# Attention scores of a 16-head layer as one matmul per head on 32-row tiles

## The reference, cut to what matters

```
mod = silu(c) @ ada_w.T + ada_b          # shifts, scales, gates
h = layernorm(x) * (1 + scale_msa) + shift_msa
q, k, v = (h @ qkv_w.T + qkv_b)          # 16 heads of 8 each
attn = einsum('bhnd,bhmd->bhnm', q, k) * 8 ** -0.5
attn = where(mask, attn, -1e9);  attn = softmax(attn)
x = x + gate_msa * (einsum('bhnm,bhmd->bhnd', attn, v) @ proj_w.T + proj_b)
x = x + gate_mlp * (gelu(modulate(layernorm(x)) @ fc1_w.T + fc1_b) @ fc2_w.T + fc2_b)
```

## Time and profile before

| | |
|---|---|
| three runs | 249.68, 250.20, 250.73 us |
| span of the profiled execution | 249.0 us |
| TensorE matmul busy | 206.9 us (83%) |
| VectorE busy | 186.8 us (75%) |
| ScalarE busy | 180.2 us (72%) |
| GpSimd busy | 163.5 us (66%) |
| granted TensorE clock | 0.998 of full speed |
| attention steps | about 72 to 213 us |

### The profile page before, as it was taken

The page is one execution under the profiler, slowest core; times in us unless marked ns, Lnnn a source line. Parts: engine busy times, 40 slices in busy tenths (PEclk is TensorE's granted clock), DMA queues, the critical chain, the costliest instruction groups (busy, mean ns, idle before and its releaser), DMA issues.

```text
span 249.0 us, 5248 instructions
## 1 busy us (share of the span) xinstructions
PE 206.9 (83%) x1596; PEld 154.1 (62%) x1596; DVE 186.8 (75%) x530; ACT 180.2 (72%) x381; POOL 163.5 (66%) x287
## 2 busy tenths in 40 slices
PE   0689998999998687977978787897888778998894
PEld 0548875678876466755746655665666556564784
DVE  0673895647199998989989989989998999058514
ACT  2147769545758788997998988989899877984330
POOL 2499589998676586875876776677689723338500
PEclk9999999999999999999999999999999999999999
DMA  6950000071000000000000000000000000000112
GB/s 159 413 219 0 4 1 0 5 295 42 0 4 0 0 3 1 4 1 0 0 0 0 0 0 0 0 0 0 0 0 3 0 0 3 0 3 0 42 42 86
DMA packets 2768, 8.28 MB, mean 33 GB/s; under 512 B 496, under 2 KB 832, under 8 KB 2496
## 3 DMA queue, kind: packets, MB, share of 16 engines
q1 hardware_dynamic: 2176, 6.22, 6.7%
q10 hardware_dynamic: 576, 1.86, 2.0%
HBM read 7.01 MB, written 1.06 MB: 32 GB/s over the span
## 4 chain that ended last, share of the span: by engine, by line
DVE 34%; PE 31%; issue 19%; ACT 6%; POOL 5%; DMA 2%; DVEq 1%; POOLq 0%; ACTq 0%
PE ps L305 8%; DVE nmax L938 7%; PE ps L295 7%; DVE kdiag L933 7%; DVE nmdiag L956 5%; PE ps L253 3%; DVE xn L781 3%; PE ps L353 2%; PE ps L241 2%; DMA xs<-x 2%; DVE nm L946 2%; PE ps L364 2%; DVE bn_c L979 2%; POOL rstd L1080 2%; DVE qk L923 2%
## 5 line engine op out<-in xcount | busy, mean ns | idle before, releaser
L665 ACT ACTIVATE qdiag<-qxT 32x512 fp32r<-32x512 f32 x64 | 40.2, 628 | 1.4
L938 DVE TENSOR_REDUCE nmax<-ps 128x8 f32<-128x1024 f32 x32 | 37.7, 1217 | 2.2 <-PE ps L353 1.6
L670 ACT ACTIVATE shared<-ps 128x1024 f32<-128x1024 f32 x32 | 31.0, 1021 | 6.6 <-PE ps L377 6.6
L353 PE MATMUL ps<-kdiag,qxT 128*128 128x512 f32 x64 | 20.5, 436 | 16.2 <-DVE kdiag L933 16.2
L1209 POOL TENSOR_TENSOR qkx<-qk,qkx 128x256 fp32r<-128x256 f32 x32 | 22.8, 734 | 16.3 <-ACT qkx L650 16.2
L1214 POOL TENSOR_TENSOR kdiag<-kxT,quarter 128x512 fp32r<-128x512 f32 x16 | 19.9, 1244 | 19.4 <-ACT kxT L659 19.4
L621 ACT ACTIVATE hid<-ps,W 128x512 f32<-128x512 f32 x32 | 21.6, 691 | 14.7 <-PE ps L295 14.6
L933 DVE CAST kdiag<-kxT 32x512 fp32r<-32x512 f32 x48 | 31.2, 651 | 1.0 <-ACT kxT L659 0.6
L305 PE MATMUL ps<-W,hid 128*128 128x128 f32 x256 | 29.9, 275 | 0.0
L305 PEld LDWEIGHTS ps<-W,hid 128*128 128x128 f32 x256 | 29.4, 192 | 0.6 <-issue 0.5
L295 PE MATMUL ps<-hT,W 128*128 128x512 f32 x64 | 29.4, 598 | 0.0
(11 more groups left out here) (148 smaller groups left out, 477.8 us busy)
## 6 DMA issues: line engine op xcount, KB each, us to landing
gate<-gates SPq DMA_DIRECT2D x1, 2048.0 KB, 6.9
xs<-x SPq DMA_DIRECT2D x4, 256.0 KB, 9.4
mask_i<-mask ACTq DMA_DIRECT2D x1, 1024.0 KB, 9.5
W<-weights SPq DMA_DIRECT2D x1, 768.0 KB, 12.0
out<-xs SPq DMA_DIRECT2D x3, 256.0 KB, 2.3
R<-rows ACTq DMA_DIRECT2D x1, 512.0 KB, 7.0
W<-weights SPq DMA_DIRECT2D x1, 512.0 KB, 10.8
W<-weights SPq DMA_DIRECT2D x1, 392.0 KB, 10.1
```

Source lines behind the costliest of these rows:

```text
L353: ins = mm(ps[:, t, :], qxT[u][:, t], kdiag[u][:, t], start=True, stop=True)
L665: ins = a(qdiag[u][rows, :, r], qxT[u][rows], ACT.Copy)
L670: a(pT[u][:, 2 * e:2 * e + 2], ps[:, 2 * e:2 * e + 2, :].rearrange("n t (r q) -> n t r q", r=4), ACT.Exp, scale=HD ** -0.5).then_inc(s["c_ ...
L938: v.tensor_reduce(nmax[u][:, 8 * e:8 * e + 8], ps[:, 2 * e:2 * e + 2, :].rearrange("n t (r k) -> n (t r) k", r=4), AX.X, ALU.max, negate=T ...
```

## The change

Each head gets a matmul of its own. The operands are the 32 rows of the head in `qxT` and `kxT` themselves, so `kdiag`, `qdiag` and `nmdiag` aren't built, and their copies, memsets and waits go. A matmul with 32 rows uses a tile of 32 rows of the array. Row group r writes to bank r (before, slice t wrote to bank t), and so the maxima, the exponentials, the v slots and the host's packing of the v bias and the projection weights take the heads in another order. All sixteen score matmuls now stand behind one wait for both halves of the exponentials of b-1; before, banks 0 and 1 waited for the first half alone, and `front_a` stood between the two halves. The four `nmdiag` copies become one copy `nmT` of 128 rows, and the subtraction's first half signals ScalarE by itself.

```
-                for t in (t for e in halves for t in (2 * e, 2 * e + 1)):
-                    if back and t % 2 == 0:
-                        pe.wait_ge(s["c_exp"], 2 * b + t // 2 - 1)
-                    ins = mm(ps[:, t, :], qxT[u][:, t], kdiag[u][:, t], start=True, stop=True)
-                    if t % 2:
-                        ins.then_inc(s["c_S"], 1)
+                if back:
+                    pe.wait_ge(s["c_exp"], 2 * b)
+                for t in range(4):
+                    for r in range(4):
+                        rows = slice(32 * r, 32 * r + 32)
+                        ins = mm(bank(r)[:, t], qxT[u][rows, t], kxT[u][rows, t], start=True, stop=True,
+                                 skip_group_check=True)
+                        if t == 3 and r % 2:
+                            ins.then_inc(s["c_S"], 1)
...
-                for t in (2 * e, 2 * e + 1):
-                    mm(ps[:, t, :], kxT[u][:, t], qdiag[u][:, t], start=True, stop=False, skip_group_check=True)
+                for t in range(4):
+                    for r in (2 * e, 2 * e + 1):
+                        rows = slice(32 * r, 32 * r + 32)
+                        mm(bank(r)[:, t], kxT[u][rows, t], qxT[u][rows, t], start=(t == 0), stop=False,
+                           skip_group_check=True)
...
+                pe.wait_ge(s["c_nmT"], b + 1)
                 for e in range(2):
-                    pe.wait_ge(s["c_nmT"], 2 * b + e + 1)
                     for t in range(4):
-                        ins = mm(bank(t)[:, 2 * e:2 * e + 2], sel[:, t], nmdiag[u][:, 2 * e:2 * e + 2], start=False,
-                                 stop=True, skip_group_check=True)
-                        if e and t % 2:
-                            ins.then_inc(s["c_ST"], 1)
+                        for r in (2 * e, 2 * e + 1):
+                            rows = slice(32 * r, 32 * r + 32)
+                            ins = mm(bank(r)[:, t], sel[rows, t], nmT[u][rows], start=False, stop=True,
+                                     skip_group_check=True)
+                    ins.then_inc(s["c_ST"], 1)
...
-                scores(b, u, (0,), back)
                 if ahead:
                     front_a(b + 2, u)
-                scores(b, u, (1,), back)
+                scores(b, u, back)
...
-            def front_qdiag(b, u, rs):
-                act.wait_ge(s["c_qT"], b + 1)
-                for r in rs:
-                    rows = slice(32 * r, 32 * r + 32)
-                    ins = a(qdiag[u][rows, :, r], qxT[u][rows], ACT.Copy)
-                ins.then_inc(s["c_qd"], 1)
...
-            def front_kdiag(b, u):
-                dve.wait_ge(s["c_kT"], b + 1)
-                for r in range(3):
-                    rows = slice(32 * r, 32 * r + 32)
-                    ins = v.tensor_copy(kdiag[u][rows, :, r], kxT[u][rows])
-                ins.then_inc(s["c_kd"], 1)
...
-                for r in range(4):
-                    rows = slice(32 * r, 32 * r + 32)
-                    ins = v.tensor_copy(nmdiag[u][rows, r], ps[rows, 4, 256:256 + N])
-                    if r % 2:
-                        ins.then_inc(s["c_nmT"], 1)
+                v.tensor_copy(nmT[u][:], ps[:, 4, 256:256 + N]).then_inc(s["c_nmT"], 1)
...
-            for m in qdiag:
-                p.memset(m[:].bitcast(F32), 0.0).then_inc(s["diag_ok"], 1)
...
-            def front_kdiag(b, u):
-                pool.wait_ge(s["c_kT"], b + 1)
-                p.tensor_tensor(kdiag[u][:, :, 3], kxT[u][:], quarter[:].unsqueeze(1).broadcast_to((128, 4, N)), ALU.mult)\
-                    .then_inc(s["c_kd3"], 1)
```

More of the change, by code:

```diff
@@ L143, in build @@
         kxT = [sb(f"kxT{u}", [128, 4, N], F32R) for u in range(2)]
-        qdiag = [sb(f"qdiag{u}", [128, 4, 4, N], F32R) for u in range(2)]
-        kdiag = [sb(f"kdiag{u}", [128, 4, 4, N], F32R) for u in range(2)]
         vx = [sb(f"vx{u}", [N, 8 * 64]) for u in range(2)]
@@ L148, in build @@
         nm = [sb(f"nm{u}", [N, 4, 32]) for u in range(2)]
-        nmdiag = [sb(f"nmdiag{u}", [128, 4, N], F32R) for u in range(2)]
+        nmT = [sb(f"nmT{u}", [128, N], F32R) for u in range(2)]
         pT = [shared[:, 4 * u:4 * u + 4] for u in range(2)]
@@ L342, in front_k, with scores @@
                 ins.then_inc(s["c_Tk"], 1)
[L344 to L349, removed]
-                for t in (t for e in halves for t in (2 * e, 2 * e + 1)):
-                    if back and t % 2 == 0:
-                        pe.wait_ge(s["c_exp"], 2 * b + t // 2 - 1)
-                    ins = mm(ps[:, t, :], qxT[u][:, t], kdiag[u][:, t], start=True, stop=True)
-                    if t % 2:
-                        ins.then_inc(s["c_S"], 1)
+            def scores(b, u, back):
+                pe.wait_ge(s["c_qT"], b + 1)
+                pe.wait_ge(s["c_kT"], b + 1)
+                if back:
[7 more added lines that the diff above has]
+                            ins.then_inc(s["c_S"], 1)
             def scores_t(b, u, e):
-                if e == 0:
-                    pe.wait_ge(s["c_kT"], b + 1)
-                    pe.wait_ge(s["c_qd"], 3 * b + 3)
                 pe.wait_ge(s["c_max"], 2 * b + e + 1)
-                for t in (2 * e, 2 * e + 1):
-                    mm(ps[:, t, :], kxT[u][:, t], qdiag[u][:, t], start=True, stop=False, skip_group_check=True)
+                for t in range(4):
[3 more added lines that the diff above has]
+                           skip_group_check=True)
             def turn_maxima(b, u):
@@ L1007, in step @@
                     statistics_1(b - 2)
-                if front:
-                    front_kdiag(b + 1, 1 - u)
                 if ahead:
@@ L1119, in _ @@
                 p.memset(nm[u][:], 0.0).then_inc(s["c_vinit"], 1)
-                p.memset(nmdiag[u][:].bitcast(F32), 0.0).then_inc(s["c_vinit"], 1)
-            pool.wait_ge(s["c_vinit"], 6)
+            pool.wait_ge(s["c_vinit"], 4)
             for u in range(2):
@@ L1166, in _, with prepare @@
                 .then_inc(s["own_ok"], 1)
-            for m in kdiag:
-                p.memset(m[:].bitcast(F32), 0.0).then_inc(s["diag_ok"], 1)
-            def prepare(b, u, end=False, last_kdiag=False):
+            def prepare(b, u, end=False):
                 settled(pool)
@@ L1232, in step @@
                 if ahead:
-                    prepare(b + 2, u, end, True)
+                    prepare(b + 2, u, end)
                 else:
@@ L1302, in columns, with heads @@
         return np.concatenate([cols, np.zeros((128, 16 - cols.shape[1]), np.float32)], axis=1)
+    def heads(rows):
+        return rows.reshape(4, 2, 2 * HD, -1).transpose(1, 0, 2, 3).reshape(rows.shape)
     packed = {
@@ L1310 @@
         "ada": l1["ada_w"].T,
-        "cols1": columns(l1["ada_b"], l1["qkv_b"][2 * C:], l1["fc1_b"]),
+        "cols1": columns(l1["ada_b"], heads(l1["qkv_b"][2 * C:]), l1["fc1_b"]),
         "qkv": l1["qkv_w"].T,
-        "proj1": l1["proj_w"].T, "fc1": l1["fc1_w"].T,
+        "proj1": heads(l1["proj_w"].T), "fc1": l1["fc1_w"].T,
         "fc2": l1["fc2_w"].T.reshape(FC, 128, C).transpose(1, 0, 2).reshape(128, F),
```

36 lines of the change are left out of this document (12 added, 24 removed).

## The result

The changed kernel takes 275.53 us (median of four runs, 270.92 to 277.10), the one before 250.24 beside it. The ratio, 1.0904 of before (95% interval 1.0816 to 1.0992), is taken from the two faster of the four, 270.92 and 274.89; with the median of all four it would be 1.10. Forecast was 243.0 with 234 to 256, so both the sign and the range are wrong. The profiled execution took 274.89 us, with a span of 273.2.

A forecast was written before the change was run, and what follows sets the result against it. VectorE was taken as the bound; relieved, a serial loop of 8.45 us a step against 8.82 remains. Savings 3.7 + 0.8 + 2.0 + 0.8 = 7.3 us give 243 us, range 234 to 256.

The forecast's parts named there:

- The bound: Attention loop before the change: VectorE, busy 16.54 of 17.60 us over two steps, sets the pace.
- Sixteen score matmuls: First scores on TensorE: side-by-side loads on four row tiles, 0.65 to 0.70 us; 1.77 if every load queues.
- Transpose to subtraction: Loop, from the start of the maxima's transpose to the subtraction's start: 1.12 us before plus 0.30 for three shape changes, 1.42.
- The step: One attention step of the loop after the change: 8.45 us against 8.82 before.
- The head: Before the loop: memsets and waits go, first maxima 1.3 us earlier at 71.95, step 1's at 81.2; gain 2.0 us.
- The end: Last step and tail: three `nmdiag` copies less at 0.29, one change of shape more; gain 0.8 us.
- The last paragraph: List of signs to check; a granted clock below full, from TensorE idling longer, would show the forecast wrong.
- the two small operations: Loop, VectorE after the maxima: high and low part of the maxima, 1.02 us.
- Rival A: Weight loads of different row groups queue on TensorE: 10.4 us a step, 272 us; chance 0.15.
- Rival B: Shape changes at 0.27 us each, or TensorE's order, eat the gain: 8.95 a step, 250 us; chance 0.15 with D.
- Rival C: Shape changes free and the two small operations 0.69 us in the loop: 7.8 a step, 235 us; chance 0.20.
- D: No effect, because VectorE wasn't the bound: 250 us; chance 0.15 together with B.

The follow-up runs named there:

- the whole filler: Changed kernel plus eight full-height 128x128 matmuls a step, result unused: four before the scores, four before the transpose of the maxima; 253.77 us, ratio 1.0114.
- half the filler: Changed kernel plus only four unused full-height matmuls a step, those before the scores; 257.44, 260.67, 270.37 and 274.51 us in four runs.
- filling the start alone: Changed kernel plus eight unused full-height matmuls a step in steps 0 and 1 only; 266.25 and 277.26 us beside 250.35.

## Why the prediction was wrong

**The bound, right.** VectorE set the step; without the copies the kernel takes 233 us.

**The loop's terms at full clock, right in the main.** Sixteen score matmuls take 0.67 us in step 0, against 0.65 to 0.70 forecast; queued would be 1.77. Loads for different row groups run side by side. Transpose to subtraction: 1.41 in step 0 (75.89 to 77.30), against 1.42; with the whole filler 1.63. The step: 8.49, 8.65 and 8.58 at full clock with half the filler, against 8.45.

**The head, a mis-sized term.** The first maxima start at 72.89, 0.33 us earlier than before and not 1.3 (71.95 was forecast). The wait for `xn` is gone, as forecast, but the copy of the transposed weights, forecast to end at 41.55, ends at 42.30, and TensorE waits 1.79 us for it. With the memsets gone GpSimd converts the mask earlier (1.90 us from 39.79), and beside it the two small VectorE operations ahead of the copy take 0.81 and 1.83 us where they took 0.16 each; that the one slows the other isn't tested. Step 1's maxima start at 81.76, against 81.2. The end, from the last step's first maxima on, is 44.5 us against 44.05 before, where 0.8 less was forecast; its first 3.3 us run at the low clock. Head and tail together are 1.8 of the 31.5 us that the forecast of the span is short.

**The step that failed** is the sum's silent premise, that every duration read before the change holds after it. The last paragraph named it ("a granted clock below full [...] it stands at 1.00 throughout now") as what would make the forecast wrong, but gave it no price, no chance and no rival. The reason it named, longer idle time, fits the first fall at most; the falls in the loop come without it, and filling the start alone didn't help. Its price can be read from the loop step above, forecast against measured: sixteen scores and their release 0.69 against 1.15, transpose of the maxima after their negation 0.15 against 1.47, transpose to subtraction 1.42 against 1.68, the two small operations 1.02 against 0.81, and 0.02 less in the release of ScalarE; together 1.81 more, 10.26 instead of 8.45. With two steps at 12.4 and twelve near 10.2, the fourteen intervals between the steps' maxima take 146.9 us (81.76 to 228.67), where the forecast had 117.2 (121.73 - 3.7 - 0.8): 29.7 of the 31.5 us between the span forecast (241.7) and the span measured. With the clock restored by filler the kernel takes 253.8, and what then stands above the forecast is in TensorE's order, 8.97 a step.

**Rival A**, 272 us, comes near the time and is refuted as a cause: it needed 1.1 us more for the scores at full clock, and they take 0.67. The forecast gave 0.15 to a case with the right size for a wrong reason. **Rival B**: the transpose starts at 75.89, the tiles behind it at 76.12, so 0.23 from start to start, beside 0.10 within one shape: a change of shape costs 0.13, near the forecast's 0.10 and not B's 0.27. B's 8.95 a step is seen only with the whole filler, which makes the transpose wait. **Rival C**: little came free. The two small operations take 0.81 in the loop and not 1.02, yet the steps at full clock take 8.2 to 8.65 with half the filler, not 7.8. **D** is refuted by the kernel without copies.

**What stays open.** The runs show that tiles of 32 rows hold the clock less well than full-height matmuls, and that it gets worse with their number. By what measure the chip decides isn't shown. Number and kind aren't separated either: 16 are always the first scores, and 32 the transposed scores and the subtraction. Nor was it tried whether the 32-column tiles of the weighted sum, which both kernels have, count in the same way.

## What to carry to other kernels

When full-height matmuls are replaced by small tiles, treat the granted clock as a term of the sum: price the stage at the low level too, as a rival with a chance. Then change the part that relieves the engine that bounds and leave the rest at full height; here a third of the tiles gave 3.3%, 5.8% with one copy moved, and all of them lost 9%. After a surprise look at the clock row of the page before any line of the timeline.

## What was not expected of the hardware

- TensorE can be busy 80 of 80 us by the records and be granted 0.52 of its clock, and the clock can fall with no pause before it (3.00 of 3 us busy from 120 us in the changed kernel); eight matmuls of 128 rows a step in place of eight of 32 rows are worth 87 us.
- At the low level the sixteen scores go from 0.67 to 1.12 us and a half of the weighted sum from 0.65 to 1.08, so 1.7 times and not twice as long, while the exponentials and maxima beside them keep 1.94 and 2.36.
- Sixteen 128-column loads and matmuls on four row tiles take 0.67 us, 0.04 each.
- The changed kernel's runs lie 6 us apart and those with half the filler 17, where the kernel before stays within 2.2 over all its runs. A kernel at the edge of a clock level can't be timed in one run.
